# First layer: V of two pairs of heads projected together in split fp32r, in the steps of each couple's first pair

## The reference, cut to what matters

```
for i in range(2):                       # two halves j of the sequence, weights of their own
    h = einsum('od,bdl->bol', Wqkv[i], z[:, :, s:e]) + einsum('od,bdl->bol', Winj[i], u[:, :, s:e])
q, k, v = split(concatenate(chunks, axis=2), 3, axis=1)
score = einsum('bndi,bndj->bnij', q + r_w_bias, k) * SCALE
prob = softmax(score)
attn_vec = einsum('bnij,bndj->bndi', prob, v)
x = einsum('od,bdl->bol', Wo, attn_vec) + bo + z
x = (x - mean(x)) * rsqrt(var(x) + eps)  # over channels
```

## Time and profile before

| | |
|---|---|
| median of 3 runs | 1374.92 us (1370.78 to 1375.06) |
| the profiled execution | 1375.67 us, of which the span of the core is 1373.8 |
| first layer's steps | from 22.5 to about 390 us |
| mean granted clock of PE | 0.973 of full speed |

### The profile page before, as it was taken

How to read it: one execution, slowest core, us unless ns; L and a number is a source line. 1 busy time by engine, 2 the same in 40 slices (tenths; PEclk the granted TensorE clock), 3 DMA queues, 4 the chain that set the end, 5 groups by cost and what they waited for, 6 DMA issues and landing times.

```text
span 1373.8 us, 24470 instructions
## 1 busy us (share of the span) xinstructions
PE 1269.7 (92%) x8912; PEld 1012.4 (74%) x8912; DVE 830.5 (60%) x1900; ACT 746.3 (54%) x2040; POOL 540.5 (39%) x571
## 2 busy tenths in 40 slices
PE   6999999999898988999999999999998977787788
PEld 5777777777644557899999889999985645545555
DVE  4666666766648976666666766666673039639510
ACT  4665656665546875555454655555543147647531
POOL 3554444544359963232130413221202039449320
PEclk9999999999997999999999999999999998988989
DMA  6101010100010004111111202020001010000000
GB/s 255 49 26 51 26 51 26 51 26 28 3 64 0 1 1 140 32 48 31 47 45 35 63 16 70 9 70 16 9 1 62 0 62 1 1 16 1 1 8 23
DMA packets 15525, 50.44 MB, mean 37 GB/s; under 512 B 1840, under 2 KB 5296, under 8 KB 14384
## 3 DMA queue, kind: packets, MB, share of 16 engines
q1 hardware_dynamic: 15408, 48.87, 10.8%
HBM read 47.82 MB, written 1.05 MB: 36 GB/s over the span
## 4 chain that ended last, share of the span: by engine, by line
PE 80%; DVE 12%; ACT 3%; issue 2%; POOL 2%; DMA 0%; SPq 0%; DVEq 0%; POOLq 0%
PE pS L1648 13%; PE acc L315 6%; PE pT L1676 6%; PE acc L1728 6%; PE pC L378 5%; PE pT L365 5%; PE pS L348 4%; PE pS L1690 4%; PE acc L334 4%; PE pC L1713 4%; DVE stats L1299 4%; PE acc L921 3%; PE pT L1452 2%; PE acc L1438 2%; PE pC L1452 2%
## 5 line engine op out<-in xcount | busy, mean ns | idle before, releaser
L1648 PE MATMUL pS<-split_sources,split_pair_weights 128*128 128x512 f32 x768 | 212.6, 412 | 5.8 <-issue 4.3
L665 POOL TENSOR_TENSOR probs<-probs,stats 128x512 f32<-128x512 f32 x128 | 130.6, 1042 | 167.0 <-DVE stats L543 166.9
L486 ACT ACTIVATE probs<-pS,stats 128x256 f32<-128x256 f32 x256 | 118.1, 473 | 111.1 <-DVE stats L538 111.1
L1648 PEld LDWEIGHTS pS<-split_sources,split_pair_weights 128*128 128x128 f32 x768 | 136.4, 191 | 30.8 <-issue 6.6
L1825 ACT ACTIVATE probsT<-pT 128x256 f32<-128x256 f32 x128 | 49.3, 385 | 197.0 <-PE pT L1701 197.0
L1728 PE MATMUL acc<-l_wo_parts,l_ctx_parts 128*128 128x256 f32 x768 | 122.0, 295 | 1.0 <-DVE l_ctx_parts L1897 1.0
L1676 PEld LDWEIGHTS pT<-l_wv_parts,split_sources 128*128 128x128 f32 x756 | 106.9, 188 | 14.2 <-issue 2.2
L1676 PE MATMUL pT<-l_wv_parts,split_sources 128*128 128x256 f32 x756 | 110.6, 281 | 2.1 <-issue 2.1
L1951 POOL TENSOR_TENSOR split_pair_weights<-weights_a,split_pair_weights 128x1024 fp32r<-128x1024 f32 x16 | 38.1, 2381 | 170.0 <-ACT split_pair_weights L1789 169.9
L315 PE MATMUL acc<-split_sources,split_pair_weights 128*128 128x512 f32 x372 | 101.9, 408 | 0.9 <-POOL split_pair_weights L652 0.7
L1728 PEld LDWEIGHTS acc<-l_wo_parts,l_ctx_parts 128*128 128x128 f32 x768 | 99.4, 190 | 1.2 <-DVE l_ctx_parts L1897 1.2
(11 more groups left out here) (206 smaller groups left out, 2979.1 us busy)
## 6 DMA issues: line engine op xcount, KB each, us to landing
weights_a<-in_l_w SPq DMA_DIRECT2D x16, 768.5 KB, 4.2
weights_a<-in_l_w SPq DMA_DIRECT2D x16, 768.0 KB, 5.9
value_bias_rows<-in_l_bv SPq DMA_DIRECT2D x16, 256.0 KB, 4.5
weights_b<-in_l_wo SPq DMA_DIRECT2D x16, 256.0 KB, 2.7
w_fc<-in_l_w SPq DMA_DIRECT2D x4, 1024.0 KB, 6.0
bias_rows<-in_rows SPq DMA_DIRECT2D x1, 1536.0 KB, 13.6
x_residual<-in_x_dbl SPq DMA_DIRECT2D x2, 512.0 KB, 7.1
masked_scores<-in_ctx_dbl SPq DMA_DIRECT2D x2, 512.0 KB, 8.0
```

The source lines that it names most:

```text
L486: a = e.activation(self.E[:, n % 4, h, it, :], self.S[h][:, it, :], ACT.Exp, bias=self.st[:, 1, n % 4, h, it:it + 1], accum_out=self.st[:, ...
L665: e.tensor_tensor(self.E[:, n % 4, h, :, :], self.E[:, n % 4, h, :, :], self.st[:, 3, n % 4, h, :].unsqueeze(2).broadcast_to([P, 2, D]), A ...
L1648: mm = e.matmul(bank[:, :], self.w_qk[i % 2][kw][:, 1 - which, c, h * P:h * P + P], g.split[:, which, ks, c, half * HALF:half * HALF + HAL ...
```

## The change

For i = 0 and 1 nothing changes: V of each unit is a plain fp32 product. From i = 2 on, the pairs are taken in couples (i = 2 and 3, 4 and 5, ..., 14 and 15). V of both pairs of a couple is made in one group of twelve fp32r matmuls with 256 columns, 128 of each pair, in the steps of the couple's first pair (`project_v_pairs`, steps 8 to 11, 24 to 27 and so on: every n with n // 4 even, from 8). It stands where `project_v(n + 4)` stood, and is for unit n and not n + 4. The steps of the couple's second pair, and steps 4 to 7, hold no V. DVE copies both pairs' values out in one instruction.

The weights of V are split as well. ACT makes the high part (`high_v_weights`) and POOL the low part (`low_v_weights`) of one i each, in the steps with n // 4 odd and n % 4 = 0 and 2. The parts lie in space that the next layer's masked keys use. ACT's high parts of the second half's sources move by one step (from 4, 6, 8, 10 to 5, 7, 9, 11), and POOL's low parts with them. `BACK_STEP` moves from 42 to 45 to 44 to 47, so that all of the bank's other users lie in steps without V. SP waits for the low part of V's weights in place of V itself.

```diff
-    BACK_STEP = [42, 43, 44, 45]
+    BACK_STEP = [44, 45, 46, 47]
+    V_SINGLE = 8
...
-                e.wait_ge(self.v_full, 4 * (i - 1))
+                if i < 4:
+                    e.wait_ge(self.v_full, 4 * (i - 1))
+                else:
+                    e.wait_ge(self.wv_lo, i - 3)
...
+    def v_step(self, n):
+        return self.V_SINGLE + 4 * (n // 8 - 1) + min(4, n % 8)
...
+        def project_v_pairs(n):
+            i, s = divmod(n, 4)
+            half = i // NPAIR
+            at = self.v_step(n)
+            b = self.UNITS * half + s
+            if s == 0:
+                e.wait_ge(self.wv_lo, i)
+            e.wait_ge(self.v_ready, at)
...
+            for j in range(2):
+                for t, (m, kw, ks) in enumerate(PARTS):
+                    mm = e.matmul(self.bV[:, j * D:j * D + D], self.zu[m][ks][:, b, j * P:j * P + P],
+                                  self.wv[kw][:, :, 2 * j + m, :], start=t == 0, stop=t == len(PARTS) - 1)
             mm.then_inc(self.v_full, 1)
...
+            if n < 4:
+                project_v(n + 4)
+            elif n >= 8 and n // 4 % 2 == 0 and n < self.N:
+                project_v_pairs(n)
             if n + 4 < self.N:
-                project_v(n + 4)
                 project_qk(n + 4)
...
+        def high_v_weights(i):
+            e.wait_ge(self.w_loaded[i % 2], 16 * (i // 2 + 1))
+            if i >= 4:
+                e.wait_ge(self.v_full, self.v_step(8 * (i // 2 - 1)) + 4)
+            e.activation(g.l0_wv[:, 0, i % 2, :], self.pack[i % 2][:, 8 * P:12 * P], ACT.Copy)\
+                .then_inc(self.wv_hi, 1)
...
+            if n // 4 % 2 == 1 and n % 4 in (0, 2) and n < self.N - 4:
+                high_v_weights(n // 4 + 1 + n % 4 // 2)
+            if n in (5, 7, 9, 11):
+                high_sources(4 + (n - 5) // 2)
...
+        def evacuate_v_pairs(n):
+            e.wait_ge(self.v_full, self.v_step(n) + 1)
+            pairs = g.v[:, :, :].rearrange("p (q s) (j n) -> p q s j n", q=2, j=2)
+            e.tensor_copy(pairs[:, :, n % 4], self.bV[:, :].rearrange("p (j q n) -> p q j n", j=2, q=2))\
+                .then_inc(self.v_ready, 1)
...
+        def low_v_weights(i):
+            e.wait_ge(self.wv_hi, i - 1)
+            e.tensor_tensor(g.l0_wv[:, 1, i % 2, :], self.pack[i % 2][:, 8 * P:12 * P],
+                            g.l0_wv[:, 0, i % 2, :].bitcast(F32), ALU.subtract).then_inc(self.wv_lo, 1)
```

More of the change, by code:

```diff
@@ L74, in __init__ @@
         self.sm = sb("masked_scores", [P, 4, 512])
-        self.km, self.wo_parts = overlay(2048, [("masked_keys", [P, 3, 512], F32)],
+        self.km, self.l0_wv, self.wo_parts = overlay(2048, [("masked_keys", [P, 3, 512], F32)],
+                                         [("l0_wv_parts", [P, 2, 2, 512], F32R)],
                                          [("l2_wo_parts", [P, 2, 2, 2 * D], F32R)])
@@ L172 @@
     SUM_STEP = [36, 37, 38, 39]
-    BACK_STEP = [42, 43, 44, 45]
+    BACK_STEP = [44, 45, 46, 47]
+    V_SINGLE = 8
+    V_STEPS = 4 * (NPAIR - 1)
     def __init__(self, g):
@@ L191, in __init__ @@
         self.w_lo = s("l0_weights_low_ready")
+        self.wv_hi, self.wv_lo = s("l0_v_weights_high_ready"), s("l0_v_weights_low_ready")
         self.qk_full = s("l0_q_k_in_bank")
@@ L230, in __init__ @@
         self.ws = [[a.rearrange("p (q m o) -> p q m o", q=2, m=4) for a in parts] for parts in self.flat_ws]
+        self.wv = [g.l0_wv[:, k, :, :].rearrange("p q (m o) -> p q m o", m=4) for k in range(2)]
         self.wo = [g.wB[:, P * i:P * i + P] for i in range(2)]
@@ L241, in __init__ @@
         self.bQ, self.bV = g.acc[2], g.acc[3]
-        self.shared_v = {n + 5: (self.f_raw, b + 1) for b, n in enumerate(self.SUM_STEP)}
-        self.shared_v |= {n + 5: (self.x_done, b + 1) for b, n in enumerate(self.BACK_STEP)}
     def load_pack(self, e, i):
@@ L323, in project_v @@
                 e.wait_ge(self.w_loaded[i % 2], 16 * (i // 2 + 1))
-            if n % (4 * NPAIR) == 0:
+            if n == 0:
                 e.wait_ge(self.z_loaded[half], 16)
@@ L328, in project_v @@
                 e.wait_ge(self.v_ready, 1 if n == 3 else n)
-            if n in self.shared_v:
-                e.wait_ge(*self.shared_v[n])
             bank, b = self.value_bank(n), self.UNITS * half + s
@@ L335, in project_v @@
                                   self.w[i % 2][:, 2, 2 * j + m, :], start=m == 0, stop=m == 1)
+            mm.then_inc(self.v_full, 1)
+        def project_v_pairs(n):
[6 more added lines that the diff above has]
+            e.wait_ge(self.v_ready, at)
+            if n == 12 * 4:
+                e.wait_ge(self.f_raw, 4)
+                e.wait_ge(self.x_done, 4)
+            if n == 10 * 4:
+                e.wait_ge(self.f_raw, 4)
+            for j in range(2):
+                for t, (m, kw, ks) in enumerate(PARTS):
+                    mm = e.matmul(self.bV[:, j * D:j * D + D], self.zu[m][ks][:, b, j * P:j * P + P],
+                                  self.wv[kw][:, :, 2 * j + m, :], start=t == 0, stop=t == len(PARTS) - 1)
             mm.then_inc(self.v_full, 1)
@@ L370, in context @@
             slot = 4 * (n // 4 % 2) + n % 4
-            e.wait_ge(self.v_ready, 4 if n < 4 else n + 1)
+            e.wait_ge(self.v_ready, 4 if n < 4 else n + 1 if n < 8 else self.v_step(8 * (n // 8) + n % 4) + 1)
             e.wait_ge(self.pt0, n + 1)
@@ L396, in sum_transposes @@
             if b < 4:
-                e.wait_ge(self.v_ready, self.SUM_STEP[b] + 5)
+                e.wait_ge(self.v_ready, self.v_step(36))
+                if b:
+                    e.wait_ge(self.f_raw, b)
             elif b < 6:
-                e.wait_ge(self.v_ready, self.N)
+                e.wait_ge(self.v_ready, self.v_step(self.N))
                 e.wait_ge(self.qk_lo, self.N)
@@ L428, in pe @@
                 if n == self.BACK_STEP[b]:
-                    e.wait_ge(self.v_ready, n + 5)
+                    e.wait_ge(self.v_ready, self.v_step(44))
+                    if b:
+                        e.wait_ge(self.x_done, b)
                     self.back_transposes(e, b)
@@ L511, in act @@
                 high_weights(n // 4 + 2)
-            if n in (4, 6, 8, 10):
-                high_sources(4 + (n - 4) // 2)
+            if n // 4 % 2 == 1 and n % 4 in (0, 2) and n < self.N - 4:
+                high_v_weights(n // 4 + 1 + n % 4 // 2)
+            if n in (5, 7, 9, 11):
+                high_sources(4 + (n - 5) // 2)
             for b in range(4):
@@ L602, in dve @@
                 evacuate_t(n - 2)
-            if n + 4 < self.N:
+            if n < 4:
                 evacuate_v(n + 4)
+            elif n >= 8 and n // 4 % 2 == 0 and n < self.N:
+                evacuate_v_pairs(n)
             if n < self.N:
@@ L689, in pool @@
                 low_weights(i, n % 4 - 1)
-            if n in (5, 7, 9, 11):
-                low_sources(4 + (n - 5) // 2)
+            if n // 4 % 2 == 1 and n % 4 in (0, 2) and n < self.N - 4:
+                low_v_weights(n // 4 + 1 + n % 4 // 2)
+            if n in (6, 8, 10, 12):
+                low_sources(4 + (n - 6) // 2)
             if n in (self.SUM_STEP[1] + 1, self.SUM_STEP[3] + 1):
```

## The result

The changed kernel takes 1363.29 us in the median of 5 runs (1361.43 to 1363.94), the kernel before 1372.81 us (1370.78 to 1375.06) in 5: 9.5 us less, a ratio of 0.9927 with a 95% interval of 0.9911 to 0.9943. A second set of the same kernel, timed for the experiments, gave 1362.99 us beside 1371.78: 8.8 us less. The forecast was 1366.0 us, 8.9 us under the median known then.

What follows compares the result with a forecast made beforehand. PE was taken to bound the first layer's steps: 50.1 us removed, 39.8 added and 1.4 lost in waits make 8.9 us less, from a median of 1374.92 to 1366.0 us, range 1361 to 1371.

Steps and rivals of the forecast that it cites:

- PE is the bound, and V's work on it is the gain: First layer's steps: the chain never leaves PE, so a microsecond less on PE is one less in the end.
- 50.1 us removed, 39.8 added: PE, first layer: V of one unit leaves 56 steps; twelve fp32r matmuls come in 28 steps; balance 10.3 us less.
- The price of 0.118 us for an fp32r matmul of 256 columns: New V on PE: each matmul costs what the third layer's V shows, so twelve cost 1.42 us.
- a moving operand in two pieces costs nothing: New V on PE: two pieces of 128 columns add nothing, judged by the queries and keys; upper bound 0.233 us each.
- The wait of the first scores: Steps 8, 16, 24, 32, 56: a new pair's scores wait for low keys, 0.28 us each, 1.4 us in all.
- the two that the transposes cover: Steps 40 and 48: transposes of the bank's other users take 0.37 us ahead of the scores and cover the wait.
- The sign to look for: Profile after: PE idle 0.3 us before the first scores of steps 8, 16, 24, 32 and 56.
- The margin at the second transposes: Steps without V: DVE's copy of probsT is ready 0.27 us ahead of PE, so no wait.
- The rival that I gave 9 in 100: Steps without V wait at the second transposes, 0.1 to 0.2 us each, 4.2 us: 1370.2; chance 9 in 100.
- The splitting costs nothing: ACT's high and POOL's low parts of V's weights fit beside the steps; ACT's have 1.0 us of cover.
- POOL blocking DVE: In-place normalisation beside POOL's weights, steps 39 to 42: POOL can block DVE for 1.0 us; charged nothing.

Runs made afterwards that it cites:

- the last experiment: Changed kernel with V of two pairs left out but for two of its twelve matmuls: 1332.10 us, ratio 0.971 to the kernel before.
- the kernel with the large reduction: Changed kernel plus one DVE reduction over 512 columns ahead of the second transposes' copy in each of 28 steps without V: 1371.05 us.

## Why the prediction was right

**PE is the bound, and V's work on it is the gain.** Shown. Less V (the last experiment) takes the time down by what its matmuls cost, but for 2.75 us in three steps, and step by step the gain is 0.89 us in steps without V and -0.53 in steps with it.

**50.1 us removed, 39.8 added.** The rows gave both, and the first layer's 9.5 us bear out the difference with the wait below: a step without V takes 4.78 us and one with V 6.20, as worked out. The price of 0.118 us for an fp32r matmul of 256 columns, carried over from the third layer, and the claim that a moving operand in two pieces costs nothing, both hold: twelve take 1.42 to 1.44 us.

**The wait of the first scores.** Right in place, cause, number and the two that the transposes cover: steps 8, 16, 24, 32 and 56 alone are late, and 40 and 48 are not. Its size was put too high, 0.28 us where 0.165 were measured, so 0.8 us in all and not 1.4. The term that was off is the start of the high keys: I let them begin when the last exponential's recorded time ends (3.68 us into the step), and ACT began them at 190.39 - 186.83 = 3.56:

```profile
190.30 0.21 ACT L525 ACTIVATION_READ_ACCUMULATOR probs<-pS,stats 128x1 f32 x1
190.39 0.61 ACT L517 ACTIVATE l_keys_parts<-acc 128x512 fp32r<-128x512 f32 x1
```

An instruction that waits for nothing starts here 0.12 us before the record of the one ahead of it ends (190.51). On DVE it is 0.08: the copy starts at 189.06, and the record of the maxima ends at 187.85 + 1.29 = 189.14. The 0.06 us from the low keys' end to the scores was right. With this the sum is 50.1 - 39.8 - 0.8 = 9.5 us, which is what the first layer shows.

**The sign to look for** was not quite right: I expected idle time of PE ahead of those scores, and the list of PE shows none, since the context product's modelled end (190.60 + 1.08 = 191.68) reaches over most of the gap before 191.78. It is seen in the starts and in the chain.

**The margin at the second transposes** was put at 0.27 us and is 0.28. What the prediction did not have is that a wait there costs 0.06 us beyond its own length. The margin decides over the change: 0.6 us more on DVE in each step without V and all of the gain is gone. The rival that I gave 9 in 100 did not come, but its mechanism is real.

**The splitting costs nothing.** Shown by doubling it. **POOL blocking DVE** costs nothing in the changed kernel, and up to 2.3 us in two steps where they are shorter. The blocked pairs take 1.57 to 1.88 us beside 0.60; the one from 234.46 ends at 236.34, with POOL's instruction, which runs from 234.98 to 236.26. The prediction read one of its rows wrongly here: it set DVE's copy of 0.68 us beside POOL's probabilities, and POOL stood idle then (the copy starts at 213.02, the probabilities at 214.18). The claim holds in the changed kernel, where the copy runs beside POOL's low weights:

```profile
188.34 1.29 POOL L714 TENSOR_TENSOR l_wv_parts<-weights_a,l_wv_parts 128x512 fp32r<-128x512 f32 x1
...
189.06 0.68 DVE L588 COPY probsT<-pT 128x512 f32<-128x512 f32 x1
```

By the Trainium skill ("SBUF — State Buffer", section "Who interferes with whom"), a DVE instruction in a two-port mode and one of GpSimd exclude each other, the first of the two for its whole length, while a DVE instruction outside these modes with at most one input in SBUF is not held up. The trace agrees with both: 1.88 us beside POOL for the pair in place, and 0.68 us with and without POOL for the copy out of PSUM.

**What stays open.** The layers behind the first took 994.5 and 994.8 us in the two profiles of the changed kernel, 998.9 before and 998.9 in the kernel with the large reduction, and 996 to 997 in the others. Both profiles with 998.9 are of a slow execution: 1375.67 us, above all timed runs of the kernel before, and 1376.22, the slowest of ten with a median of 1371.05. So the spread looks like one between executions and not like work of the change. The later part's granted clock differs with it, 0.97 and 0.96, but what decides it was not tried. The forecast's absolute time lay 2.7 us above the result; 2.1 us of this is the median of the kernel before, 1374.92 in 3 runs and 1372.81 in 5, and 0.6 is the wait of the first scores, put too high.

## What to carry to other kernels

Before a plain fp32 product is replaced by three fp32r parts, price the matmul at the number of columns it will have. Here, with weight loads of 128 columns, 128 moving columns lost 21 us and 256 gained 9. To get more columns, put what two iterations share into one group. Then look at the steps that this empties: they are shorter than the mean, so the next engine has less slack there. Measure it in them (here 0.28 us). And compare whole lists of starts, since a wait of 0.17 us in five steps shows neither as idle time nor in the timing.

## What the runs showed of the hardware that was not expected

An fp32r matmul of 128 columns with a weight load of its own takes 0.108 us, one of 256 columns 0.118, one of 512 0.233: from 256 columns to 128 the cost falls by a tenth only. V between the context product and the scores takes 1.62 us in place of 1.42. The weights' shape changes on both sides of it there, which may be the cause, but no run shows this apart. Transposes that had waited for a copy took 0.06 us longer to give way to the next product than those that had not (0.59 against 0.53).
